# Experts of layers 1 and 3: results gathered in eight pieces over two queues, constant products in two gaps of TensorE, bias additions signalled one by one

## The chip, the cores and the metric

The kernel runs on one core of one Trainium2 chip. The metric is the device time of a whole execution in microseconds (us); each kernel is timed in several executions, and the median is quoted. The engines are named as in the profile: PE is TensorE (matmuls; PEld are its weight loads), DVE is VectorE, ACT is ScalarE, POOL is GpSimd, and SP is the sync engine, which here only issues transfers. SPq is SP's own sequence of transfer issues.

## What is computed

The program is a four-layer perceiver. Each layer has cross-attention, self-attention and a feed-forward part, each added to the token matrix `x` (1024 tokens of 256 numbers). The change touches the feed-forward parts of layers 1 and 3, which are mixtures of experts:

```python
def _L1_ffn_ref(x, gate_w, gate_b, w1, b1, w3, b3, w2, b2, sw1, sb1, sw3, sb3, sw2, sb2):
    def swiglu(x):                       # even and odd columns
        g = jnp.minimum(x[..., ::2], 7.0); l = jnp.clip(x[..., 1::2], -7.0, 7.0)
        return g * jax.nn.sigmoid(1.702 * g) * (l + 1.0)
    scores = jax.nn.softmax(xt @ gate_w.T, axis=-1)
    _, idx = jax.lax.top_k(scores + gate_b, 2)
    ...
    # each chosen expert, weighted with its score:
    h = swiglu((xt @ ew1 + eb1) * (xt @ ew3 + eb3))
    acc + ce[:, None] * (h @ ew2 + eb2)
    # and for every token the shared expert:
    shared = swiglu((xt @ sw1 + sb1) * (xt @ sw3 + sb3)) @ sw2 + sb2
```

Layer 3 has six experts of the form `gelu(x @ W1 + b1) @ W2 + b2`, two for each token, with weights from a softmax over the two largest gate values.

## The kernel before

The 1024 tokens are 8 tiles of 128 rows (`NT = 8`). One class, `SortedExperts`, holds the expert parts of layers 0, 1 and 3. It sorts the (token, expert) pairs by expert into tiles of 128 rows that each belong to one expert, runs the tiles one after the other, stores each tile's result row by row into a matrix in HBM (`out_dram`, by an indirect transfer from POOL), and at the end loads that matrix back in the order of the tokens (`gathered`). In layers 1 and 3 a token has K = 2 results, which PE sums with diagonal matrices of the weights (`sum_pairs`). Layer 1 (names `l1f_...`, kind `swiglu`) has 8 turns for the shared expert (n = 0 to 7, S = 8) and then 23 sorted tiles; layer 3 (`l3f_...`, kind `gelu`) has sorted tiles alone. Layer 0 (`l0f_...`, kind `glu`) has K = 1. Three sets of buffers (`RING = 3`) rotate.

Every engine runs its own instructions in the order in which the code writes them, and semaphores join them. There is no planner. The parts that matter:

- PE, `tensor`: each turn transposes the next tile's rows, multiplies with the first matrices (`up`, L1034; in layer 1 two halves u = 0 and 1 of 32 recorded matmuls each, every half with its own wait), and then does the last product of the turn before (`down`, L1045). The first half of `up` waits for `gate_done` of the turn before, the second for its `hidden_done`. After the loop one `down` is left, and then `sum_pairs` (L1070) sums the pairs of tokens' tiles, g = 0 to 3, each waiting for its own part of the gather.
- ACT, `scalar`: for kind `swiglu` and each half, four additions of a bias (L1111, `side`, 128x128 each), after which one semaphore step tells DVE that all four are done; then the sigmoid (L1116).
- DVE, `vector`: four products (L1155) that read PE's result and `side`, then `gated` (L1160) for u = 0, or L1162, L1163 and `hidden` (L1166) for u = 1. It copies the result of `down` out (L1138), and after the last turn adds the sums to `X` (L1185); in layer 1 it takes the statistics of the next normalization behind each.
- SP, `load`: the experts' weights, two transfers for a tile, and after the last three stores have landed the gather in four transfers (L970), each of 128 x 4 x 256 numbers, that is 512 KB. In layer 3 SP then stores the output in four parts (L3731).
- `keep_busy(bank, n)` (L81) issues n products of constants of 256 columns on PE, whose result nobody reads. At the two places of this change there are none before.

A matmul of 32-bit floats is recorded twice, so that a call of `nc.tensor.matmul` is two records.

## Time and profile before

| | us |
|---|---|
| median of three executions | 2022.7 |
| lowest and highest | 2019.74, 2023.64 |
| the profiled execution, its own time | 2023.79 |
| the profiled execution, its span | 2022.0 |
| PE busy in the span | 1821.4 (90%) |
| DVE, ACT, POOL busy | 1083.4, 815.1, 546.6 |

All times of rows are microseconds from the start of the span. The profile has a page of totals; the trace behind it gives the instructions in order of time (timeline), the waits by pair, and sums over chosen stretches. A timeline row has start, duration, engine, line, operation, what it writes and reads, how many records it merges, and in brackets how long the engine sat idle before it and what released it. A duration of several records is from the start of the first to the end of the last. In rows of stretches, "PEclk" is the granted clock of PE as a share: 1.00 is 2.4 GHz and 0.50 is 1.2 GHz. The page's chain of the work that ended last names many lines of all layers with 1% of the span or less each, so it points to no single one.

### The profile page before, as it was taken

Reading aid. Unit: us, or ns where it says so; the run is one execution under the profiler, and the core shown is the slowest. Engines: PE = TensorE matmul, PEld = TensorE weight load, DVE = VectorE, ACT = ScalarE, POOL = GpSimd, SP = SyncE. Lnnn points to the kernel's source line nnn. Section 1 sums busy time; section 2 is a strip of 40 time slices with the busy share of each in tenths; the row PEclk is TensorE's granted clock in tenths of the full one; section 3 lists DMA queues with packets and bytes.
Section 4 is the critical chain, followed back from the end, with each engine's and each line's share of the span. In section 5 each row is a group of like instructions: output and inputs, shape, how many; then the busy total and the mean of one; then the engine's idle time right before and its main releaser. Section 6 shows DMA issues by size and latency. Waiting matters only on the chain. (4 is left out here: it accounts for less than half of the span.)

```text
span 2022.0 us, 42986 instructions
## 1 busy us (share of the span) xinstructions
PE 1821.4 (90%) x16746; PEld 1409.5 (70%) x16746; DVE 1083.4 (54%) x2711; ACT 815.1 (40%) x2356; POOL 546.6 (27%) x598
## 2 busy tenths in 40 slices
PE   8999779999999888899999799996688899996887
PEld 6886569745777746799999667775444577664786
DVE  7887841451466348675555445557733655355411
ACT  6663521131366243233333245552501566525231
POOL 4441213100244113201121023331202466412241
PEclk9999779999999999999999899998788999997898
DMA  4210069560243000143989331111102355200396
GB/s 142 59 50 4 3 237 319 169 206 31 66 102 101 16 41 3 52 173 131 332 331 333 131 131 49 49 33 43 40 15 68 104 156 157 64 1 2 120 341 224
DMA packets 86882, 233.93 MB, mean 116 GB/s; under 512 B 9648, under 2 KB 45008, under 8 KB 80176
## 3 DMA queue, kind: packets, MB, share of 16 engines
q1 hardware_dynamic: 81040, 216.01, 31.9%
q0 software_dynamic: 5664, 15.47, 2.4%
q8 instruction: 120, 1.97, 0.4%
q14 instruction: 58, 0.48, 0.1%
HBM read 216.23 MB, written 12.07 MB: 113 GB/s over the span
## 5 line engine op out<-in xcount | busy, mean ns | idle before, releaser
L2166 POOL TENSOR_TENSOR l1x_probs<-l1x_probs,l1x_total 128x512 f32<-128x512 f32 x64 | 65.1, 1038 | 209.5 <-DVE l1x_total L2391 209.5
L1487 PE MATMUL PS<-weights,l0x_ctxT 128*128 128x256 f32 x512 | 121.6, 388 | 0.0
L1034 PE MATMUL PS<-l1f_xT,l1f_slot 128*128 128x128 f32 x1024 | 117.0, 275 | 0.0
L1034 PEld LDWEIGHTS PS<-l1f_xT,l1f_slot 128*128 128x128 f32 x1024 | 115.7, 192 | 0.1
L1487 PEld LDWEIGHTS PS<-weights,l0x_ctxT 128*128 128x128 f32 x512 | 94.6, 191 | 15.4 <-issue 2.7
L2898 POOL TENSOR_TENSOR l2x_probs<-l2x_probs,l2x_total 128x512 f32<-128x512 f32 x64 | 65.1, 1038 | 137.2 <-DVE l2x_total L3072 137.2
L235 ACT ACTIVATE std<-moments,eps 128x8 f32<-128x8 f32 x13 | 3.9, 301 | 220.5 <-DVEq L173 135.3
L81 PE MATMUL PS<-consts 128*128 128x256 f32 x276 | 73.9, 423 | 16.1 <-PEq L87 16.1
L81 PEld LDWEIGHTS PS<-consts 128*128 128x128 f32 x276 | 57.8, 214 | 28.7 <-issue 19.9
L1155 DVE SCALAR_TENSOR_TENSOR l1f_product<-PS,l1f_slot,l1f_side 128x128 f32<-128x128 f32 x128 | 36.0, 344 | 65.9 <-ACT l1f_side L1111 65.9
L3362 PE MATMUL PS<-l3x_keysT,l3x_QW 128*128 128x289 f32 x256 | 67.7, 407 | 1.7 <-issue 1.7
L3222 PE MATMUL PS<-weights,HT 128*128 x128 | 59.5, 620 | 9.5 <-DVE X L3255 9.5
L988 POOL DMA_INDIRECT l1f_out_dram<-l1f_out,l1f_sort_target_row x23 | 22.7, 986 | 162.1 <-DVE l1f_out L1138 162.1
L1034 PE MATMUL PS<-HT,weights 128*128 128x128 f32 x512 | 61.5, 282 | 2.2 <-DVE l1f_hidden L1166 1.3
L1034 PEld LDWEIGHTS PS<-HT,weights 128*128 128x128 f32 x512 | 60.5, 198 | 3.2 <-DVE l1f_hidden L1166 1.7
L2925 PE MATMUL PS<-l2x_ctxT,weights 128*128 128x257 f32 x256 | 62.3, 387 | 0.0
L3386 PE MATMUL PS<-tagged,l3x_QT 128*128 128x256 f32 x256 | 60.6, 379 | 1.9 <-ACT tagged L3471 1.9
L1155 DVE SCALAR_TENSOR_TENSOR l1f_product<-PS,weights,l1f_side 128x128 f32<-128x128 f32 x120 | 33.8, 344 | 52.5 <-ACT l1f_side L1111 52.5
L1667 ACT ACTIVATE l0x_sq<-PS 128x256 f32<-128x256 f32 x128 | 47.8, 385 | 32.6 <-PE PS L1487 32.6
L2933 PE MATMUL PS<-weights,l2x_ctxT 128*128 128x256 f32 x256 | 60.4, 379 | 0.0
L3018 ACT ACTIVATE l2x_probs<-PS,l2x_top 128x257 f32<-128x257 f32 x128 | 59.2, 482 | 1.6 <-DVE l2x_top L3066 1.3
L2208 PE MATMUL PS<-HT,weights 128*128 128x512 f32 x128 | 57.3, 608 | 2.2 <-DVE l1x_AT L2355 2.2
(659 smaller groups left out, 4652.6 us busy)
## 6 DMA issues: line engine op xcount, KB each, us to landing
l1f_slot<-in_experts_up_dram SPq DMA_DIRECT2D x16, 2056.0 KB, 10.3
weights<-in_experts_up_dram SPq DMA_DIRECT2D x8, 2056.0 KB, 10.6
weights<-in_experts_down_dram SPq DMA_DIRECT2D x21, 640.0 KB, 5.8
weights<-in_experts_up_dram SPq DMA_DIRECT2D x10, 1024.0 KB, 7.8
l1f_slot<-in_experts_down_dram SPq DMA_DIRECT2D x16, 640.0 KB, 5.2
l0x_ctxT<-in_ctxT_dram SPq DMA_DIRECT2D x32, 257.0 KB, 2.6
l1x_ctxT<-in_ctxT_dram SPq DMA_DIRECT2D x32, 257.0 KB, 3.0
l2x_ctxT<-in_ctxT_dram SPq DMA_DIRECT2D x32, 257.0 KB, 2.6
```

The source lines that it names most:

```text
L81: self.nc.tensor.matmul(self.PS[:, bank, 0:2 * P], self.ident, self.consts[:, 0:2 * P], start=True, stop=True)
L1034: done = nc.tensor.matmul(PS[:, bank + a, m * P:(m + 1) * P], mat[:, c, m * P:(m + 1) * P], x, start=(c == 0), stop=(c == 1))
L1155: done = nc.vector.scalar_tensor_tensor(p[:, m, :], PS[:, 2 * u + 1, m * P:(m + 1) * P], w["b3"][:, 4 * u + m:4 * u + m + 1], self.side[u] ...
L1487: last = nc.tensor.matmul(PS[:, 2 * (b % 2) + k, half * D:(half + 1) * D], ctxT[b % SLOTS][:, c, half * P:(half + 1) * P], kw[:, c, k * D: ...
L2166: nc.gpsimd.tensor_tensor(p, p, bcast(total[b % 2][:, 2 * n:2 * n + 2], 2, KEYS), ALU.mult).then_inc(probs_done, 1)
L2898: nc.gpsimd.tensor_tensor(p, p, bcast(total[b % 2][:, 2 * n:2 * n + 2], 2, 2 * P), ALU.mult).then_inc(probs_done, 1)
L2925: last = nc.tensor.matmul(PS[:, 4 + 2 * o, 0:CTX], wk[:, c, o * P:(o + 1) * P], ctxT[b % 2][:, c, :], start=(c == 0), stop=(c == 1))
L2933: last = nc.tensor.matmul(PS[:, 5, half * D:(half + 1) * D], ctxT[b % 2][:, c, half * P:(half + 1) * P], wv[:, c, :], start=(c == 0), stop ...
L3018: done = nc.scalar.activation(probs[b % 2][:, u, :], PS[:, u, 0:CTX], ACT.Exp, bias=top[b % 2][:, u:u + 1], scale=-1.0, accum_out=total[b ...
L3222: last = nc.tensor.matmul(PS[:, t % 4, :], core.HT[:, c, t * P:(t + 1) * P], experts[:, c, bass.ds(i * (2 * D), 2 * D)], start=(c == 0), s ...
L3362: done = nc.tensor.matmul(PS[:, 2 * (b % 2) + u, 0:KEYS], QW[:, c, b, 4 * u:4 * u + 4, :].rearrange("p h q -> p (h q)"), keysT[b % 2][:, c ...
L3386: nc.tensor.matmul(PS[:, 6 + c, 0:2 * P], tokens[b % 2][:, half, c * P:(c + 1) * P], probsT[b % 2][:, half, :], start=(half == 0), stop=False)
```

## The change

Four things are changed. The gather is issued as eight transfers of one token tile each in layers 1 and 3 (two of the matrix's 128-row blocks, 256 KB), the even ones by SP and the odd ones by ACT, which has a queue of its own; both first wait for the last three stores. `sum_pairs` waits for each token tile instead of each pair of tiles. PE issues 5 constant products before the last `down` of layer 1, and 12 before `sum_pairs` in both layers, into bank 5. ACT signals each of the four bias additions, and DVE waits for each before the product that reads it. Layer 0 keeps its four transfers of 256 KB from SP.

```diff
-        self.gather_done = [sem(f"gather_done{g}") for g in range(4)]
+        self.gather_done = [sem(f"gather_done{g}") for g in range(4 * choices)]
...
+        self.gather_rows(sp, range(0, NT, 2) if self.K == 2 else range(NT // 2))
+
+    def gather_rows(self, eng, parts):
+
+        by_token = self.out_dram[0:self.K * NT * P, :].rearrange("(n p) d -> p n d", p=P)
         for n in range(self.N - RING, self.N):
-            sp.wait_ge(self.stored[n % RING], 16 * self.nth(*divmod(n, RING)))
-        by_token, n = self.out_dram[0:self.K * NT * P, :].rearrange("(n p) d -> p n d", p=P), 2 * self.K
-        for g in range(NT // 2):
-            sp.dma_start(self.gathered[:, n * g:n * (g + 1), :], by_token[:, n * g:n * (g + 1), :]).then_inc(self.gather_done[g], 16)
+            eng.wait_ge(self.stored[n % RING], 16 * self.nth(*divmod(n, RING)))
+        for g in parts:
+            eng.dma_start(self.gathered[:, 2 * g:2 * (g + 1), :], by_token[:, 2 * g:2 * (g + 1), :]).then_inc(self.gather_done[g], 16)
...
-        self.over(pe, lambda: S or flip_rows(0, 0), turn, lambda: down(*divmod(self.N - 1, RING), False))
+        def finish():
+            if self.kind == "swiglu":
+                self.core.keep_busy(5, 5)
+            down(*divmod(self.N - 1, RING), False)
+
+        self.over(pe, lambda: S or flip_rows(0, 0), turn, finish)
         if self.K == 2:
+            self.core.keep_busy(5, 12)
             self.sum_pairs(pe)
...
-            pe.wait_ge(self.gather_done[g], 16)
             for t in (2 * g, 2 * g + 1):
+                pe.wait_ge(self.gather_done[t], 16)
...
-                        done = nc.scalar.activation(self.side[u][:, m, :], PS[:, 2 * u, m * P:(m + 1) * P], ACT.Identity, bias=w["b1"][:, 4 * u + m:4 * u + m + 1])
-                    done.then_inc(self.side_done, 1)
+                        nc.scalar.activation(self.side[u][:, m, :], PS[:, 2 * u, m * P:(m + 1) * P], ACT.Identity,
+                                             bias=w["b1"][:, 4 * u + m:4 * u + m + 1]).then_inc(self.side_done, 1)
...
-                    dve.wait_ge(self.side_done, 2 * n + (u + 1))
                     for m in range(4):
+                        dve.wait_ge(self.side_done, 8 * n + (4 * u + m + 1))
```

`ex.gather_rows(act, range(1, NT, 2))` is written at the end of ACT's program in `l1_feed_forward` (behind `norm.load_table`) and in `l3_feed_forward` (behind `ex.scalar`).

The order of instructions shows where these stand. Line numbers of the kernel after are 4 or 10 higher than those of before; the names of semaphores in brackets are those of their first users, since their numbers are used again by later layers.

PE at the end of layer 1's experts, before:

```order
L1045 MATMUL PS<-l1f_slot,l1f_hidden 128x256 [waits l0x_x_copied,l0x_q_flipped,l0x_q_shifted]
L1045 MATMUL PS<-l1f_slot,l1f_hidden 128x256 x3
L1045 MATMUL PS<-l1f_slot,l1f_hidden 128x256 [waits l0x_x_rows,l0x_q_flipped,l0x_q_shifted]
L1045 MATMUL PS<-l1f_slot,l1f_hidden 128x256 x3
L1070 MATMUL PS<-l1f_gathered,l1f_diagonal 128x256 [waits l0x_q_copied,l0x_scale_ready]
L1070 MATMUL PS<-l1f_gathered,l1f_diagonal 128x256 x3
L1070 MATMUL PS<-l1f_gathered,l1f_diagonal 128x256 [waits l0x_att_done]
L1070 MATMUL PS<-l1f_gathered,l1f_diagonal 128x256 x3
```

and the same place after:

```order
L1049 MATMUL PS<-l1f_slot,l1f_hidden 128x256 [waits l0x_x_copied,l0x_q_flipped,l0x_q_shifted]
L1049 MATMUL PS<-l1f_slot,l1f_hidden 128x256 x3
L81 MATMUL PS<-consts 128x256 x5
L1049 MATMUL PS<-l1f_slot,l1f_hidden 128x256 [waits l0x_x_rows,l0x_q_flipped,l0x_q_shifted]
L1049 MATMUL PS<-l1f_slot,l1f_hidden 128x256 x3
L81 MATMUL PS<-consts 128x256 x12
L1080 MATMUL PS<-l1f_gathered,l1f_diagonal 128x256 [waits l0x_q_copied,l0x_scale_ready]
L1080 MATMUL PS<-l1f_gathered,l1f_diagonal 128x256
L1080 MATMUL PS<-l1f_gathered,l1f_diagonal 128x256 [waits l0x_att_done]
L1080 MATMUL PS<-l1f_gathered,l1f_diagonal 128x256
```

The constant products wait for nothing and stand ahead of the two waiting products; a pair sum now waits before every second of its matmuls instead of every fourth. In layer 3 the end is the same without the five products.

DVE in the first shared turn of layer 1, before:

```order
L1155 SCALAR_TENSOR_TENSOR l1f_product<-PS,weights,l1f_side 128x128 [waits l0x_q_scaled,l1f_shared_biased]
L1155 SCALAR_TENSOR_TENSOR l1f_product<-PS,weights,l1f_side 128x128 x3
L1160 TENSOR_SCALAR l1f_gated<-l1f_product 128x512 [waits dve_step]
L1155 SCALAR_TENSOR_TENSOR l1f_product<-PS,weights,l1f_side 128x128 [waits l0x_q_scaled,l0x_left_done]
L1155 SCALAR_TENSOR_TENSOR l1f_product<-PS,weights,l1f_side 128x128 x3
```

and after:

```order
L1165 SCALAR_TENSOR_TENSOR l1f_product<-PS,weights,l1f_side 128x128 [waits l0x_q_scaled,l1f_shared_biased]
L1165 SCALAR_TENSOR_TENSOR l1f_product<-PS,weights,l1f_side 128x128 [waits l0x_q_scaled] x3
L1170 TENSOR_SCALAR l1f_gated<-l1f_product 128x512 [waits dve_step]
L1165 SCALAR_TENSOR_TENSOR l1f_product<-PS,weights,l1f_side 128x128 [waits l0x_q_scaled,l0x_left_done]
L1165 SCALAR_TENSOR_TENSOR l1f_product<-PS,weights,l1f_side 128x128 [waits l0x_q_scaled] x3
```

Each of the four products now has its own wait on the count of the bias additions; nothing changed its place. In the turns that run as a loop (18 of the 23 sorted tiles) each wait also has a register operation ahead of it.

ACT at the end of layer 1's experts, after (before, the branch follows the second row):

```order
L218 ACT_TABLE_LOAD
L218 ACTIVATE warm<-eps 128x1 [waits eps_set]
L974 DMA l1f_gathered<-l1f_out_dram 128x2x256 [waits l0x_left_zeroed,l0x_one_ready,l0x_left_ready]
L974 DMA l1f_gathered<-l1f_out_dram 128x2x256 x3
L2739 UNCONDITIONAL_BRANCH
```

The four issues of ACT stand behind all of its other work of the layer, with the same three waits that SP has.

## Rows read from the trace of the kernel before

**Rows 1.** Stretches: width, PE, PEld, DVE, ACT, POOL busy (records), PEclk, transfers' share, GB/s

```profile
1100.00:1120.00 20.00, 20.00 (x167) 19.49 (x166) 11.31 (x29) 6.57 (x20) 1.97 (x2) 1.00 0.92 347
1138.50:1141.30 2.80, 2.80 (x7) 1.69 (x6) 0.00 (x0) 0.00 (x0) 0.67 (x1) 0.50 0.13 47
```

**Rows 2.** Timeline of the shared turns 0 and 1 in layer 1: DVE and PE

```profile
857.98 1.13 DVE L1155 SCALAR_TENSOR_TENSOR l1f_product<-PS,weights,l1f_side 128x128 f32<-128x128 f32 x4 [1.90 <-ACT l1f_side L1111]
861.08 3.84 PE L1034 MATMUL PS<-HT,weights 128*128 128x128 f32 x32 [0.35 <-DVE l1f_hidden L1166]
865.85 1.13 DVE L1155 SCALAR_TENSOR_TENSOR l1f_product<-PS,weights,l1f_side 128x128 f32<-128x128 f32 x4
867.50 3.84 PE L1034 MATMUL PS<-HT,weights 128*128 128x128 f32 x32 [0.85 <-DVE l1f_gated L1160]
869.23 1.12 DVE L1155 SCALAR_TENSOR_TENSOR l1f_product<-PS,weights,l1f_side 128x128 f32<-128x128 f32 x4 [1.79 <-ACT l1f_side L1111]
872.33 3.84 PE L1034 MATMUL PS<-HT,weights 128*128 128x128 f32 x32 [0.99 <-DVE l1f_hidden L1166]
```

**Rows 3.** Timeline from the last turn of layer 1 to its last statistics

```profile
1133.11 1.89 PE L1045 MATMUL PS<-l1f_slot,l1f_hidden 128*128 128x256 f32 x8
1133.31 1.14 ACT L1111 ACTIVATE l1f_side<-PS,l1f_slot 128x128 f32<-128x128 f32 x4
1134.55 1.12 DVE L1155 SCALAR_TENSOR_TENSOR l1f_product<-PS,l1f_slot,l1f_side 128x128 f32<-128x128 f32 x4 [2.05 <-ACT l1f_side L1111]
1138.02 3.29 PE L1045 MATMUL PS<-l1f_slot,l1f_hidden 128*128 128x256 f32 x8 [3.02 <-DVE l1f_hidden L1166]
1144.54 2.03 SPq L970 DMA_DIRECT2D l1f_gathered<-l1f_out_dram  x4
1148.24 9.07 PE L1070 MATMUL PS<-l1f_gathered,l1f_diagonal 128*128 128x256 f32 x32 [6.92 <-DMA l1f_gathered<-l1f_out_dram]
1152.03 0.69 DVE L1185 TENSOR_TENSOR X<-PS,X 128x512 f32<-128x512 f32 x1 [10.25 <-PE PS L1070]
...
1158.86 0.25 DVE L206 BATCH_NORM_AGGREGATE moments<-stats 128x2 f32<-128x6 f32 x2
```

**Rows 4.** Timeline of the end of layer 3

```profile
2000.19 1.97 PE L1045 MATMUL PS<-weights,l3f_hidden 128*128 128x256 f32 x8 [0.56 <-issue]
2005.38 2.03 SPq L970 DMA_DIRECT2D l3f_gathered<-l3f_out_dram  x4
2009.48 8.54 PE L1070 MATMUL PS<-l3f_gathered,l3f_diagonal 128*128 128x256 f32 x32 [7.33 <-DMA l3f_gathered<-l3f_out_dram]
```

**Rows 5.** Gather of layer 1: issue to landing; stretches before the pair sums end

```profile
DMA to landing us min/median/max: 3.6/5.6/7.2
...
1145.50:1152.50 7.00, 4.26 (x11) 3.45 (x12) 0.47 (x1) 0.00 (x0) 0.00 (x0) 0.53 0.90 301
1148.30:1151.90 3.60, 3.60 (x9) 2.85 (x10) 0.00 (x0) 0.00 (x0) 0.00 (x0) 0.50 1.00 331
```

**Rows 6.** The page's group of DVE's products in layer 1: busy us, mean ns | idle before

```profile
L1155 DVE SCALAR_TENSOR_TENSOR l1f_product<-PS,l1f_slot,l1f_side 128x128 f32<-128x128 f32 x128 | 36.0, 344 | 65.9 <-ACT l1f_side L1111 65.9
```

**Rows 7.** Timeline of a late sorted turn of layer 1

```profile
1117.09 7.31 PE L1034 MATMUL PS<-l1f_xT,l1f_slot 128*128 128x128 f32 x64
1118.93 0.69 DVE L1166 TENSOR_TENSOR l1f_hidden<-l1f_product,l1f_sigmoid 128x512 f32<-128x512 f32 x1
```

**Rows 8.** Constant products at full clock, timeline of PE ahead of layer 1's experts

```profile
834.89 1.46 PE L81 MATMUL PS<-consts 128*128 128x256 f32 x6
```

**Rows 9.** Two other gaps of PE and the clock in and after them

```profile
1899.30 2.06 PE L816 MATMUL PS<-l3f_sort_marked,l3f_gathered 128*128 128x42 f32 x10 [2.29 <-DVE l3f_gathered L809]
...
1899.30:1902.00 2.70, 2.70 (x14) 2.70 (x15) 2.70 (x15) 0.00 (x0) 0.00 (x0) 0.57 1.02 347
838.67 2.95 PE L262 MATMUL PS<-consts,tagged 128*128 128x128 f32 x16 [2.32 <-DVE tagged L186]
...
838.60:840.90 2.30, 2.23 (x12) 1.39 (x12) 2.30 (x8) 0.59 (x1) 2.01 (x5) 1.00 0.98 281
```

More of the change, by code:

```diff
@@ L2788, in _ @@
             norm.load_table(act)
+            ex.gather_rows(act, range(1, NT, 2))
         @block.vector
@@ L3762, in _ @@
             ex.scalar(act)
+            ex.gather_rows(act, range(1, NT, 2))
         @block.vector
```

## The prediction

> **What bounds the kernel now.** I read the stretches first. Inside layer 1's experts PE is the bound: in a late stretch of 20 us it is busy for all 20, at the full clock [rows 1]. So a signal that reaches DVE earlier is worth nothing there; I look for places where PE itself waited. The timeline has two kinds. In the shared turns 0 to 2 of layer 1 PE stood still three times, for 0.35, 0.85 and 0.99 us, each time for a result of DVE that hangs on ACT's bias additions [rows 2]. And at the end of each expert part PE stands in an open chain: last hidden values, last down product, its copy and store, gather, pair sums [rows 3, 4]. In layer 1 PE waited 3.02 us for the hidden values, then did the last down product in 3.29 us, where the same product took 1.89 us one turn before [rows 3]; the granted clock was 0.50 in that stretch [rows 1], that is 1.2 GHz instead of 2.4. Then it waited 6.92 us for the gather and summed in 9.07 us, again at 0.50 for most of the first half [rows 3, 5]. Layer 3 is the same at the end, with a last down product at full speed (1.97 us), a wait of 7.33 us and sums of 8.54 us [rows 4]. Layer 0 is left as it is.
>
> **Part 1, bias additions one by one, shared turns.** ACT's four additions take 1.14 us and DVE's four products 1.12 us, one behind the other [rows 3]. When each product waits only for its own addition, the last one starts where the first starts now and the other three lie beside ACT: the last product now starts (4 - 1) x 0.26 us behind the first (1.12 less the 0.34 of one, over three steps [rows 6]), so each chain that begins with PE is shorter by 0.78 us. The first stall of PE (0.35) needs 0.35 of that and goes whole. The second waits for `gated` of turn 1, whose chain began behind DVE's sorting work without any idle time [rows 2], so it takes over the 0.78 of the turn before: 0.85 shrinks to 0.07, and the running gain is 0.78. The third waits for `hidden` of turn 1, behind a sigmoid that is 0.78 earlier and a product row that again waited for ACT [rows 2]: the chain is 1.56 earlier, PE's own first half only 0.78, so 0.78 of the 0.99 goes. Running gain **1.56 us**. Bounds: 0.35, if only the first stall goes, and 2.19, all three. I take 1.56, since it follows from the chain. After this PE never waits until the last turn, so what is won is kept. Cost in the sorted turns: in the row of a late turn `hidden` was done at 1119.62 (1118.93 + 0.69), and PE needs it at the second half of `up`, 1117.09 + 3.6 = 1120.7 [rows 7]. That slack of 1.1 us, plus the 0.78, covers four waits with their register operations per half.
>
> **Part 2, last turn of layer 1.** The same 0.78 us comes off the chain from ACT's additions (1133.31) to the down product (1138.02) [rows 3]. Here nothing hides it: **0.78 us** (bounds 0 and 0.78).
>
> **Part 3, five constant products before the last down product.** Six records took 1.46 us [rows 8] and eight took 1.89 [rows 3], so a record costs 0.215 us at the full clock. Five calls are ten records, 2.15 us, from 1134.84 (1133.11 + 8 x 0.215) to 1137.0. The hidden values release PE at 1138.02 - 0.78 = 1137.24. They fit, with 0.25 us to spare; if the price is off or the wait shorter they delay the product by what is over. The product should then run as layer 3's does after a short wait, in 1.97 us [rows 4] instead of 3.29: **1.32 us** (bounds 0, the clock falls all the same, and 1.40, the 1.89 of a turn before).
>
> **Part 4, twelve constant products before the pair sums.** 24 records are 5.16 us and begin right behind the last down product, so they end well inside waits of 6.92 and 7.33 us [rows 3, 4]: they delay nothing. They leave PE idle for 6.92 - 5.16 = 1.8 us in layer 1 and 7.33 - 5.16 = 2.2 in layer 3. If the clock holds, the pair sums take 1.89 + 24 x 0.215 = 7.05 us: 9.07 - 7.05 = 2.02 and 8.54 - 7.05 = 1.49. Two things could be late next. The transfers: the fourth issue began at about 1146.1 (four in 2.03 us from 1144.54 [rows 3]), and its part landed some 7.2 us later, at 1153.3 [rows 5], 8.8 us behind the first issue; the sums would start 3.7 us after the issue (1148.24 - 1144.54), and end 10.75 after it, so the last pair (1.89 us) needs its data at 8.9. That just fits. And DVE: its work from the first addition to the last statistics took 7.08 us [rows 3]; it can start 3.70 + 1.89 after the issue, and ends at 12.7 instead of 14.57 (1159.11 - 1144.54). So layer 1 keeps **1.9 us** and layer 3, where DVE only adds, **1.5 us**. Bounds for each: 0 (the clock falls in the gap) and these.
>
> **Part 5, eight pieces on two queues.** The wait per token tile lets PE begin when 256 KB are there. But with two queues pieces 0 and 1 start together, and the 16 engines of the transfers are full while the gather flows: share 1.00 at 331 GB/s, 301 over its whole length [rows 5]. If they share evenly, each of two pieces lands when the old 512 KB did: gain 0. If piece 0 comes first, up to half a part: 256 KB at 301 GB/s is 0.87 us, in each layer. I take **0**; the last pair of pieces ends at the same time either way. SP's issues took 2.03 us for four parts [rows 3], and they were over (1146.57) long before the data (1152.5) [rows 5], so a second issuer shortens nothing at the end. ACT's own work of the layer is over when it comes to its issues, and nothing is queued behind them but the next layer. The Trainium skill speaks of this in "DMA: Bandwidth & Descriptors": under "Issuing engines are not separate DMA queues" it says that transfers started by several engines run on the same 16 and only the issuing time is saved, and under "Queues, rings and completion order" that each of these engines takes turns between the queues, packet by packet. The share of 1.00 agrees with the first; no run here shows the second. By these the gain of part 5 is 0, and by the row alone it is open between 0 and 0.87.
>
> **Sum.** 1.56 + 0.78 + 1.32 + 1.9 + 1.5 = 7.06 us. The profiled execution had a time of 2023.8 us and a span of 2022.0; with this it would have 2016.7 and 2014.9. The median of the runs shown is 1.1 us lower than the profiled time, 2022.7, and from that I forecast **2015.7 us**.
>
> **The rivals.**
>
> A. *The clock falls in the gap that the twelve products leave* (the products do not do what they are for). PE's gaps of this size went both ways: after 2.32 us at 838.67 the clock stayed 1.00, after 2.29 us at 1899.30 it was at 0.57 on average in the next 2.7 us [rows 9]. Layer 3's gap of 2.2 us is of that size, layer 1's 1.8 us shorter. One fall in layer 3 costs 1.5, one in layer 1 up to 1.9: 2017.2, 2017.6, and 2019.1 for both.
>
> B. *Pieces come staggered and the sums start early.* 0.87 us more in each layer, as far as transfers and DVE let it through: 7.06 + 1.7 = 8.8, **2013.9 us**. For it: SP and ACT can issue a little apart. Against: full engines.
>
> C. *Single waits do not overlap.* If DVE's products each pay more than ACT's pace, the chains of parts 1 and 2 shorten by little; with the lower bounds 0.35 and 0 the sum is 5.1, **2017.6 us**. Against it: DVE's products are 0.34 us long at a pace of 0.26, ACT's pace is 0.26 too.
>
> D. *Slower: two queues of 1 KB packets get in each other's way.* ACT's queue is used nowhere before, so no row prices it. Parts 1 to 3 bring 3.66 us. The change turns slower when each gather's end moves back by over 1.83 us; slower by over 0.2% (4.05 us) when by 3.9. With the rate halved to 150 GB/s the 2.1 MB need 14 us instead of 7, and the last piece lands 7 us later; against sums that now end 4.0 us behind the last landing (1157.3 - 1153.3) and then 1.9 behind, each layer loses 4.9: 2022.7 + 9.8 - 3.66 = **2028.8 us**. Against it: POOL's stores ran beside SP's loads in the stretch of 347 GB/s [rows 1].
>
> **Chances and range.** 0.2% is 4.05 us, about what a measurement of this kernel can tell from no change. The forecast (2015.7, both clocks held) 0.47; A 0.25; B 0.12; C 0.10; D 0.06. The range takes in A with both falls below and B above: 2013.9 to 2019.1, and a little at the lower end, because every shift in time changes where elsewhere the clock falls, and the three executions before differ by 3.9 us: **2012.5 to 2019.2**. A, B and C, but for A with both falls at once together with such a shift, all stay over 4.05 us faster: faster 0.84, within 0.2% 0.12, slower 0.04.
>
> **What would show it right or wrong.** (1) The three stalls in the shared turns: 0, about 0.1 and 0.2 us. (2) DVE's four products start about 0.4 us behind ACT's first addition instead of 1.24. (3) The last down product of layer 1 at 1.9 to 2.0 us, right behind constant products that end before it is released, PEclk 1.00. (4) Pair sums of about 7.05 us in both layers, first one 3.6 to 4.1 us after the first issue, clock 1.00; 8.5 to 9 us would be A. (5) From the first issue to the last landing 8.8 us as before; over 10.6 would be D, and a first landing at under 3.2 us B. It would be wrong if PE had new waits in the sorted turns of layer 1, or if the clock changed its falls in other layers by more than what is won.

## The result and the profile after

The changed kernel ran at a median of 2014.49 us (8 executions, 2009.49 to 2016.19) against 2021.45 for the kernel before (8 executions, 2019.52 to 2025.42): 6.96 us less. The ratio is 0.9963, with a 95% interval of 0.9950 to 0.9976. The profiled execution took 2014.46 us with a span of 2012.7.

The timeline of the shared turns of layer 1, PE only (start, duration, engine, line, what it writes and reads, records, idle time before and what ended it), answers [rows 2]:

```profile
857.65 0.33 PE L735 MATMUL PS<-l1f_chosen,consts 128*128 128x64 f32 x2
...
858.04 7.36 PE L1038 MATMUL PS<-HT,weights 128*128 128x128 f32 x64
865.24 1.89 PE L1049 MATMUL PS<-weights,l1f_hidden 128*128 128x256 f32 x8
867.84 3.84 PE L1038 MATMUL PS<-HT,weights 128*128 128x128 f32 x32 [0.70 <-DVE l1f_gated L1170]
871.90 3.84 PE L1038 MATMUL PS<-HT,weights 128*128 128x128 f32 x32 [0.22 <-DVE l1f_hidden L1176]
875.57 1.89 PE L1049 MATMUL PS<-weights,l1f_hidden 128*128 128x256 f32 x8
```

The first stall is gone: 64 records stand in one row. The other two are 0.70 and 0.22 us. From the product of L735, which stands behind turn 0's `up`, to the down product of turn 1 it is 17.92 us. The same two points in the timeline of the kernel before are 19.46 us apart (the second row is turn 0's down product):

```profile
856.54 0.33 PE L735 MATMUL PS<-l1f_chosen,consts 128*128 128x64 f32 x2
...
864.75 1.89 PE L1045 MATMUL PS<-weights,l1f_hidden 128*128 128x256 f32 x8
...
876.00 1.89 PE L1045 MATMUL PS<-weights,l1f_hidden 128*128 128x256 f32 x8
```

The end of layer 1's experts answers [rows 3]:

```profile
1134.36 1.89 PE L1049 MATMUL PS<-l1f_slot,l1f_hidden 128*128 128x256 f32 x8
1134.56 1.14 ACT L1121 ACTIVATE l1f_side<-PS,l1f_slot 128x128 f32<-128x128 f32 x4 [0.92 <-PE PS L1038]
1135.03 1.13 DVE L1165 SCALAR_TENSOR_TENSOR l1f_product<-PS,l1f_slot,l1f_side 128x128 f32<-128x128 f32 x4 [2.05 <-ACT l1f_side L1121]
...
1136.09 2.32 PE L81 MATMUL PS<-consts 128*128 128x256 f32 x10
...
1138.51 1.97 PE L1049 MATMUL PS<-l1f_slot,l1f_hidden 128*128 128x256 f32 x8
...
1140.31 5.34 PE L81 MATMUL PS<-consts 128*128 128x256 f32 x24
...
1143.71 1.92 SPq L974 DMA_DIRECT2D l1f_gathered<-l1f_out_dram  x4
1143.73 2.02 ACTq L974 DMA_DIRECT2D l1f_gathered<-l1f_out_dram  x4
1146.79 3.69 PE L1080 MATMUL PS<-l1f_gathered,l1f_diagonal 128*128 128x256 f32 x16 [1.13 <-DMA l1f_gathered<-l1f_out_dram]
...
1150.74 3.72 PE L1080 MATMUL PS<-l1f_gathered,l1f_diagonal 128*128 128x256 f32 x16 [0.27 <-DMA l1f_gathered<-l1f_out_dram]
...
1156.02 0.25 DVE L206 BATCH_NORM_AGGREGATE moments<-stats 128x2 f32<-128x6 f32 x2
```

DVE's first product starts 0.47 us behind ACT's first addition, where it was 1.24. The constant products end just before the last down product, which now takes 1.97 us. PE's gap (idle time) before the sums is 1.13 us, and the sums run at full speed with one wait of 0.27 for a piece. The end of layer 3 answers [rows 4]:

```profile
1994.49 5.34 PE L81 MATMUL PS<-consts 128*128 128x256 f32 x24
...
1997.87 1.92 SPq L974 DMA_DIRECT2D l3f_gathered<-l3f_out_dram  x4
...
2001.52 7.14 PE L1080 MATMUL PS<-l3f_gathered,l3f_diagonal 128*128 128x256 f32 x32 [1.69 <-DMA l3f_gathered<-l3f_out_dram]
```

Stretches of the changed kernel (busy times of PE, PEld, DVE, ACT, POOL, then the granted clock, the transfers' share and GB/s), and the landing times of layer 1's gather, answer [rows 1] and [rows 5]:

```profile
1100.00:1120.00 20.00, 20.00 (x166) 19.49 (x165) 11.33 (x29) 6.94 (x21) 1.97 (x2) 1.00 0.92 351
1134.00:1142.00 8.00, 7.90 (x39) 6.73 (x38) 3.70 (x9) 2.63 (x6) 1.75 (x2) 1.00 0.06 19
...
1147.00:1154.00 7.00, 6.73 (x31) 5.61 (x31) 4.54 (x13) 0.00 (x0) 0.00 (x0) 1.00 0.61 203
2001.50:2008.50 7.00, 6.98 (x32) 5.99 (x32) 2.08 (x3) 0.00 (x0) 0.00 (x0) 1.00 0.82 271
...
DMA to landing us min/median/max: 2.9/5.5/7.0
```

The clock is 1.00 in each of these stretches. Place by place, in us, each number the difference of two starts or ends in the rows above and in [rows 2 to 4]:

| stretch | before | after | difference | forecast |
|---|---|---|---|---|
| shared turns, L735 to the down product of turn 1 | 19.46 | 17.92 | -1.54 | -1.56 |
| last turn of layer 1, ACT's first addition to the last down product | 4.71 | 3.95 | -0.76 | -0.78 |
| that down product | 3.29 | 1.97 | -1.32 | -1.32 |
| layer 1, first issue of the gather to the last statistics | 14.57 | 12.56 | -2.01 | -1.9 |
| layer 3, first issue of the gather to the end of the sums | 12.64 | 10.79 | -1.85 | -1.5 |
| sum | | | -7.48 | -7.06 |

The column of the kernel before is one profile, the same one that the forecast was made from. The spans differ by 9.3 us, so 1.8 us of this pair of profiles lies elsewhere. It is a balance of three parts. Up to L735 the changed kernel is 1.1 us later. In the sorted turns of layer 1 it loses 1.7 us. From the last statistics of layer 1 to the gather of layer 3 it gains 4.7 us, of which 2.9 are shorter waits of PE for the weights of layer 3's experts. The waits of that stretch by pair (total us, times, longest), first before, then after:

```profile
PE PS L1034 <- DMA weights<-in_experts_up_dram: 5.6, 4, 2.2
PE PS L1034 <- DMA l3f_slot<-in_experts_up_dram: 1.3, 2, 0.9
```

```profile
PE PS L1038 <- DMA weights<-in_experts_up_dram: 2.0, 5, 1.0
PE PS L1038 <- DMA l3f_slot<-in_experts_up_dram: 2.0, 2, 1.3
```

The 1.7 us that layer 1 loses are a fall of the clock, in the down product behind the narrow product of L816 (46 columns). The same stretch, first before, then after:

```profile
897.00:900.30 3.30, 3.30 (x24) 3.09 (x24) 1.47 (x6) 2.81 (x9) 0.00 (x0) 1.00 0.00 0
```

```profile
897.00:900.30 3.30, 3.30 (x8) 2.57 (x9) 2.24 (x6) 1.82 (x7) 0.00 (x0) 0.50 0.00 0
```

PE is busy all the time in both, but does 8 records instead of 24. Up to this point the two programs differ in their signals alone. The fall stands in 4 of the 14 profiles of this document. All 4 have single signals, but so have 11 of the 14, so whether the signals make it likelier can't be told.

### The profile page after: what moved, and what is told of

It is laid out like the page before. It is cut to its first block and busy times, and to the rows that moved or that the text cites. A ratio compares the mean times of both kernels' runs of the same rounds, so it can differ in the third digit from the quotient of the medians.

```text
span 2012.7 us, 43220 instructions
## 1 busy us (share of the span) xinstructions
PE 1827.7 (91%) x16804; PEld 1416.5 (70%) x16804; DVE 1084.5 (54%) x2711; ACT 815.4 (41%) x2356; POOL 547.6 (27%) x598
## 3 DMA queue, kind: packets, MB, share of 16 engines
q8 instruction: 120, 1.97, 0.4%
## 5 line engine op out<-in xcount | busy, mean ns | idle before, releaser
L81 PE MATMUL PS<-consts 128*128 128x256 f32 x334 | 85.9, 412 | 15.9 <-PEq L87 15.9
L81 PEld LDWEIGHTS PS<-consts 128*128 128x128 f32 x334 | 68.0, 207 | 29.7 <-issue 19.7
L1121 ACT ACTIVATE l1f_side<-PS,l1f_slot 128x128 f32<-128x128 f32 x128 | 36.5, 368 | 66.0 <-PE PS L1038 66.0
```

The lines of the kernel that those rows point to most:

```text
L81: self.nc.tensor.matmul(self.PS[:, bank, 0:2 * P], self.ident, self.consts[:, 0:2 * P], start=True, stop=True)
```

## The experiments

Three groups of four kernels ran, each group on one chip with its own runs of the kernel before: 2021.13 (22 executions), 2020.82 (16) and 2020.22 us (25). I call the stretch from the first issue of the gather to the last statistics of layer 1 E1, and that from the first issue to the end of the sums of layer 3 E3; they stand in the table above with 14.57 and 12.64 before and 12.56 and 10.79 after. The median of the changed kernel differed by up to 3.5 us between groups, so a part worth 2 us is read from its stretch and only checked by the median. One more number shows why. If the five stretches of the table are taken out of a profile's span, the rest should be the same for all kernels. Over the 14 profiles it went from 1959.3 to 1972.8 us: 1967.3 and 1966.7 in the two of the kernel before, 1962.5 to 1966.1 in the three of the changed kernel. A profile's own total therefore says nothing about a part of 1 to 4 us.

### The changed kernel again

No edit.

> The changed kernel once more, as the yardstick of this group. If what it gains lies at the places of the change, the pair sums of layers 1 and 3 again take 7.1 to 7.7 us at full clock and the last down product of layer 1 takes 1.97 us, while the falls of the clock in other places stand elsewhere than in the first profile. If instead the gain was a lucky position of the clock, the time is back near 2019 to 2022. My theory: 2013 to 2016 us, about 7 us under the kernel before.

2015.14 us (7 executions), ratio 0.9961 (0.9947 to 0.9974). E1 was 12.54 and E3 10.90, the gaps before the sums 1.66 and 1.61 us. E1 and E3 repeat to 0.1 us.

### Without the twelve constant products

```diff
         if self.K == 2:
-            self.core.keep_busy(5, 12)
             self.sum_pairs(pe)
```

> The changed kernel without the twelve constant products before the pair sums (layers 1 and 3); everything else stays. Theory (the products keep the clock up through the wait for the gather): PE idles about 6.3 us, the clock falls, the first half of the pair sums runs at 1.2 GHz, and the sums take 8.5 to 9.1 us in both layers instead of 7.7 and 7.1; 1.4 to 2 us are lost in each, some 3 us in all: about 3 us over the changed kernel. Rival (the pieces' earlier landing is what counts, the clock recovers anyway): under 1 us is lost.

2020.21 us (12 executions), 5.1 over the changed kernel of the group; the ratio to the kernel before is 0.9996 (0.9986 to 1.0006). Timeline and a stretch of this kernel:

```profile
1142.81 9.25 PE L1079 MATMUL PS<-l1f_gathered,l1f_diagonal 128*128 128x256 f32 x32 [6.79 <-DMA l1f_gathered<-l1f_out_dram]
1999.21 9.42 PE L1079 MATMUL PS<-l3f_gathered,l3f_diagonal 128*128 128x256 f32 x32 [6.83 <-DMA l3f_gathered<-l3f_out_dram]
...
1142.80:1147.00 4.20, 4.19 (x10) 3.36 (x11) 0.40 (x1) 0.00 (x0) 0.00 (x0) 0.50 1.05 345
```

The sums start at 1.2 GHz and take 9.25 and 9.42 us; E1 is 14.60 and E3 13.03, 2.1 us more in each, 4.2 in all, where 3 was expected. The expectation was right in kind and too low in size. Whether the finer pieces still give something without the products depends on the profile they are held against: the kernels with four pieces and no products had E1 and E3 of 14.57 and 12.64, of 16.21 and 13.90, and of 14.91 and 13.40 (the first profile of the kernel before, its second and that of the signals alone, both below). Two things don't close. The profiled execution took 2014.52 us, the lowest of the 12, in spite of its long sums, because the rest of its span was short (1961.1). And by the places this kernel keeps 3.3 us of the gain (7.5 less 4.2), where the median keeps 0.9 and its interval at most 2.8. What the other executions lost beyond the places was not profiled.

### One signal for four bias additions

```diff
-                        nc.scalar.activation(self.side[u][:, m, :], PS[:, 2 * u, m * P:(m + 1) * P], ACT.Identity,
-                                             bias=w["b1"][:, 4 * u + m:4 * u + m + 1]).then_inc(self.side_done, 1)
+                        done = nc.scalar.activation(self.side[u][:, m, :], PS[:, 2 * u, m * P:(m + 1) * P], ACT.Identity, bias=w["b1"][:, 4 * u + m:4 * u + m + 1])
+                    done.then_inc(self.side_done, 1)
...
-                    for m in range(4):
-                        dve.wait_ge(self.side_done, 8 * n + (4 * u + m + 1))
+                    dve.wait_ge(self.side_done, 2 * n + (u + 1))
+                    for m in range(4):
```

> The changed kernel with one signal behind four bias additions again, and DVE waiting once for all four. Theory: PE's three stalls in the shared turns come back (0.35, 0.85, 0.99 us; with the change 0, 0.70, 0.22), and the last turn's chain is 0.78 us longer: 2.3 us over the changed kernel, 1.54 of it between the first shared turn and the third, and nothing in the sorted turns. Rival (single waits cost in the sorted turns, with their register operations, and give part of the gain back): the sorted turns become shorter without them, and the loss is under 1 us.

2016.19 us (9 executions), 1.05 over the changed kernel. The timeline of the shared turns, PE:

```profile
855.41 0.33 PE L735 MATMUL PS<-l1f_chosen,consts 128*128 128x64 f32 x2
...
859.94 3.84 PE L1038 MATMUL PS<-HT,weights 128*128 128x128 f32 x32 [0.35 <-DVE l1f_hidden L1176]
...
866.37 3.84 PE L1038 MATMUL PS<-HT,weights 128*128 128x128 f32 x32 [0.86 <-DVE l1f_gated L1170]
871.20 3.84 PE L1038 MATMUL PS<-HT,weights 128*128 128x128 f32 x32 [1.00 <-DVE l1f_hidden L1176]
874.88 1.89 PE L1049 MATMUL PS<-weights,l1f_hidden 128*128 128x256 f32 x8
```

All three stalls are back, and from 855.41 to 874.88 it is 19.47 us, as in the kernel before. In the last turn the down product starts 4.72 us behind ACT's first addition:

```profile
1132.18 1.14 ACT L1121 ACTIVATE l1f_side<-PS,l1f_slot 128x128 f32<-128x128 f32 x4
1136.90 1.97 PE L1049 MATMUL PS<-l1f_slot,l1f_hidden 128*128 128x256 f32 x8 [0.87 <-DVE l1f_hidden L1176]
```

So the part is worth 1.54 + 0.77 = 2.3 us at its places. The median shows 1.05 of it; with 7 and 9 executions the rest is within what the remainder of the span moves. E1 and E3 stayed at 12.52 and 10.85: the sums' gain does not hang on the signals.

### Four pieces from one queue

```diff
-        self.gather_rows(sp, range(0, NT, 2) if self.K == 2 else range(NT // 2))
+        self.gather_rows(sp, range(NT // 2))
...
-            eng.dma_start(self.gathered[:, 2 * g:2 * (g + 1), :], by_token[:, 2 * g:2 * (g + 1), :]).then_inc(self.gather_done[g], 16)
+            eng.dma_start(self.gathered[:, n * g:n * (g + 1), :], by_token[:, n * g:n * (g + 1), :]).then_inc(self.gather_done[g], 16)
...
-            for t in (2 * g, 2 * g + 1):
-                pe.wait_ge(self.gather_done[t], 16)
+            pe.wait_ge(self.gather_done[g], 16)
+            for t in (2 * g, 2 * g + 1):
```

> The changed kernel with the gather as before: four transfers of 512 KB, all from SP, and one wait for each pair of token tiles; constant products and single signals stay. Theory (the transfers' engines are full, so pieces and queues change only the start): the sums begin 3.7 us (layer 1) and 4.1 us (layer 3) behind the first issue instead of 3.1 and 3.65, and end at most 0.5 us later than with eight pieces; the total is 0.3 to 1 us higher than that of the changed kernel. The idle time of PE ahead of the sums grows to about 1.8 and 2.2 us, and in one or the other the clock may fall, which would add 1.5 to 1.9 us. Rival (two queues move the data faster): the sums end 1.5 us later or more in each layer with the clock at 1.00.

2014.64 us (7 executions), as the changed kernel in the group (2015.14), so by the median the finer pieces and the second queue gave nothing. But the profiled execution (2016.2 us) shows what can happen. Timeline and stretches:

```profile
1144.54 8.83 PE L1081 MATMUL PS<-l1f_gathered,l1f_diagonal 128*128 128x256 f32 x32 [2.05 <-DMA l1f_gathered<-l1f_out_dram]
...
2001.59 8.83 PE L1081 MATMUL PS<-l3f_gathered,l3f_diagonal 128*128 128x256 f32 x32 [2.29 <-DMA l3f_gathered<-l3f_out_dram]
...
1142.00:1144.50 2.50, 0.48 (x3) 0.08 (x1) 0.00 (x0) 0.00 (x0) 0.00 (x0) 1.00 0.99 323
1144.90:1148.00 3.10, 3.10 (x9) 2.48 (x8) 0.07 (x1) 0.00 (x0) 0.00 (x0) 0.51 1.04 342
```

The sums begin 4.0 and 4.2 us behind the first issue, PE's gap is 2.05 and 2.29 us, and the clock, 1.00 in the gap, is at 0.51 once the sums have begun. E1 is 14.63 and E3 13.07: both parts of the gain in the sums are gone in this execution, with the twelve products in place. The expectation of an end at most 0.5 us later failed here, and the fall that it allowed for one layer came in both. How often that happens in the other executions the median can't tell: the 4.3 us would be hidden by what the rest of the span moves, and no second profile was taken.

### Four pieces with sixteen constant products

```diff
-            self.core.keep_busy(5, 12)
+            self.core.keep_busy(5, 16)
```

on top of the four pieces.

> Four pieces of 512 KB from SP as in the run with four pieces, but 16 constant products before the pair sums instead of 12, so that PE's gap is 0.3 to 0.6 us instead of 2.05 and 2.29. Theory (what was lost with four pieces was the clock, which fell in those gaps): the clock stays at 1.00, the sums take 7.05 to 7.2 us instead of 8.83 in both layers, and end 11.1 to 11.4 us behind the first issue, 0.3 to 0.6 later than with eight pieces. Rival (the pair wait and the late start cost, not the clock): the sums end at 12.8 to 13.1 again.

```profile
1149.01 7.14 PE L1081 MATMUL PS<-l1f_gathered,l1f_diagonal 128*128 128x256 f32 x32 [0.32 <-DMA l1f_gathered<-l1f_out_dram]
2009.50 7.14 PE L1081 MATMUL PS<-l3f_gathered,l3f_diagonal 128*128 128x256 f32 x32 [0.33 <-DMA l3f_gathered<-l3f_out_dram]
```

With gaps of 0.32 and 0.33 us the sums take 7.14 us; E1 is 12.94 and E3 11.16. So what four pieces had lost was the clock, and four pieces at full clock are 0.3 to 0.4 us slower than eight in each layer, by the later first landing. The total, 2018.37 us (11 executions, 2012.94 to 2023.00; ratio 0.9984, 0.9970 to 0.9998), is some 4 us above what the changed kernel's ratio would give, and the places explain 0.7 of it. In the profiled execution (2022.44 us) the rest of the span took 1972.8 us, the longest of all profiles, at a granted clock of 0.949 over the whole span against 0.954 in the changed kernel's first profile. Why this kernel was slower elsewhere is open.

### Eight pieces from one queue

```diff
-        self.gather_rows(sp, range(0, NT, 2) if self.K == 2 else range(NT // 2))
+        self.gather_rows(sp, range(NT) if self.K == 2 else range(NT // 2))
...
-            ex.gather_rows(act, range(1, NT, 2))
```

> The changed kernel with all eight pieces of 256 KB issued by SP, in order, ACT issuing none. Theory (the transfers' engines are full, a second queue only saves issue time): eight issues of some 0.47 us take 3.8 us, still under the 7 us of the data; piece 0 is no longer mixed with piece 1, so the sums begin as early as with two queues or 0.2 to 0.5 us earlier (2.9 to 3.6 us behind the first issue), and end within 0.3 us of 10.75 us behind it. Total within 1 us of the changed kernel. Rival (the second queue is what made it work): first landing at 3.7 us or later, or waits inside the sums, 1 us or more slower in each layer.

2009.94 us (5 executions). The timeline at layer 1:

```profile
1138.50 3.97 SPq L974 DMA_DIRECT2D l1f_gathered<-l1f_out_dram  x8
1141.34 1.97 PE L1080 MATMUL PS<-l1f_gathered,l1f_diagonal 128*128 128x256 f32 x8 [0.88 <-DMA l1f_gathered<-l1f_out_dram]
...
1143.53 5.45 PE L1080 MATMUL PS<-l1f_gathered,l1f_diagonal 128*128 128x256 f32 x24 [0.23 <-DMA l1f_gathered<-l1f_out_dram]
```

The first sum starts 2.84 us behind the first issue, 0.2 us earlier than the earliest start with two queues. E1 was 12.28 and E3 10.52. The second run tells whether this stands:

> The kernel with all eight pieces from SP again, beside the changed kernel on the same chip. In the first run the sums ended 10.5 us behind the first issue in both layers against 10.75 to 10.9 with two queues, which is 0.5 to 0.7 us in all, but the medians of two different groups differed by 4 to 5 us. Theory: the difference at the two places is 0.6 us, the rest was the clock in other places: this kernel 0 to 2 us under the changed kernel. Rival (two queues cost something elsewhere): 3 us or more under it again.

2012.56 us (12 executions) beside 2011.67 for the changed kernel. E1 was 12.69 and E3 11.02, both 0.1 to 0.2 above the changed kernel. So ACT's queue is neither a gain nor a loss that can be seen: E1 12.3 to 12.7 and E3 10.5 to 11.0 with one queue, 12.5 to 12.6 and 10.8 to 10.9 with two. The 4 to 5 us by which the first median lay lower did not repeat; in its profile the rest of the span was the shortest of all (1959.3).

### Fourteen constant products

```diff
-            self.core.keep_busy(5, 12)
+            self.core.keep_busy(5, 14)
```

> The changed kernel with 14 constant products before the pair sums instead of 12. They take 6.0 us and leave gaps of 0.3 to 0.9 us where 12 leave 1.1 to 1.7. Theory (gaps of up to 1.7 us don't let the clock fall, or seldom): sums of 7.1 to 7.7 us as before, no gain in the median, within 1 us of the changed kernel. Rival (in a part of the unprofiled executions the clock does fall in these gaps): the median is 0.5 to 1.5 us lower and the spread smaller.

The gaps were 0.51 and 0.68 us, the sums 7.14 and 7.34, E1 12.26 and E3 10.84: no gain at the places beyond 0.3 us, since with twelve the clock had held as well. Of 5 executions (2010.27 to 2021.3, median 2010.74) the spread is too wide to say whether the median is lower. The profiled one was the slowest, 2021.3, with every place of the change at full clock: its rest of the span took 1972.6 us.

### Without the five constant products

```diff
         def finish():
-            if self.kind == "swiglu":
-                self.core.keep_busy(5, 5)
             down(*divmod(self.N - 1, RING), False)
```

> The changed kernel without the five constant products before layer 1's last down product. With single signals PE's gap there is 3.02 - 0.78 = 2.2 us. Theory: this is about the size at which the clock fell with four pieces (2.05 and 2.29), so it falls in some executions and not in others; where it falls, the last down product takes up to 3.3 us instead of 1.97, where not, 1.97. In the median 0.5 to 1.3 us over the changed kernel. Rival: the shorter gap alone is enough, and nothing is lost.

2013.09 us (6 executions, 2008.95 to 2018.28). In the profiled execution the last down product took 1.97 us:

```profile
1133.81 1.97 PE L1049 MATMUL PS<-l1f_slot,l1f_hidden 128*128 128x256 f32 x8 [2.25 <-DVE l1f_hidden L1174]
```

The gap of 2.25 us did not let the clock fall there. The next kernel has the same gap:

### The signals alone, in the kernel before

The edit of the single signals, as in the change, and nothing else.

> The kernel before with one part of the change alone: each bias addition signalled and waited for by itself, nothing else. Theory: the stretch from the start of layer 1's experts to the end of their last turn becomes 2.3 us shorter where the clock is the same (1.54 in the shared turns, 0.78 in the last turn), the sorted turns keep 9.1 us each, and PE's wait before the last down product goes from 3.02 to 2.2 us, so the clock may stay up there in some executions. Total 2 to 3 us under the kernel before. Rival (of the 7 us of the change this part gives only what the whole medians differ by, 1 us): 2019.5 to 2020.5 us.

2017.02 us (12 executions), 3.2 under the kernel before in its group; ratio 0.9986 (0.9974 to 0.9998). From L735 to the down product of turn 1 it was 17.93 us and in the last turn's chain 3.95, as in the changed kernel, so the 2.3 us are there without anything else of the change. The sums, without products, took 9.19 and 9.24 us, E1 14.91 and E3 13.40. At the last down product:

```profile
1138.62 3.07 PE L1045 MATMUL PS<-l1f_slot,l1f_hidden 128*128 128x256 f32 x8 [2.25 <-DVE l1f_hidden L1166]
...
1138.70:1141.60 2.90, 2.90 (x8) 1.92 (x8) 0.00 (x0) 0.00 (x0) 0.97 (x1) 0.61 0.13 45
```

The same gap of 2.25 us behind the same work, and here the clock fell and the product took 3.07 us. So for a gap of about 2 us its length alone does not decide, and the five products are an insurance worth up to 1.1 us (3.07 less 1.97) once the signals are single, not a fixed gain.

### The yardsticks of the last group

> The changed kernel once more, as the yardstick of this group: 2010 to 2017 us, 6 to 8 us under the kernel before.

2011.67 us (8 executions), ratio 0.9963 (0.9950 to 0.9975); E1 12.61, E3 10.79, gaps 1.72 and 1.69.

> The kernel before, one more profile. The last down product of layer 1 again at about 3.3 us, pair sums of 8.5 to 9.1 us in both layers, and from the last turn of layer 1 to the first work of the next layer 21 us as in the first profile. The places where the clock falls elsewhere, and the waits of layer 3's sorted tiles for weights, may lie otherwise: where they do, they are not of the change.

One execution, 2026.35 us. Its places, from the timeline:

```profile
1142.01 3.62 PE L1045 MATMUL PS<-l1f_slot,l1f_hidden 128*128 128x256 f32 x8 [3.03 <-DVE l1f_hidden L1166]
1153.12 10.16 PE L1070 MATMUL PS<-l1f_gathered,l1f_diagonal 128*128 128x256 f32 x32 [7.48 <-DMA l1f_gathered<-l1f_out_dram]
...
2010.95 9.62 PE L1070 MATMUL PS<-l3f_gathered,l3f_diagonal 128*128 128x256 f32 x32 [7.50 <-DMA l3f_gathered<-l3f_out_dram]
```

The down product took 3.62 us, the sums 10.16 and 9.62: E1 was 16.21 and E3 13.90, 1.6 and 1.3 us above the first profile. Of the 1.6 us in layer 1, 0.55 are a later start of the sums (4.25 us behind the first issue instead of 3.70) and 1.09 longer sums. The expectation (3.3, and 8.5 to 9.1) was too narrow. Without the products, the end of the experts does not have one price; with twelve or fourteen products and eight pieces E1 was 12.3 to 12.7 in all eight profiles.

## Why the prediction was right, point by point

The forecast was 2015.7 us from 2022.7, a gain of 7.0; measured were 6.96, and 6.0 to 8.6 in the other two groups. The first median of before was 1.25 us above the one of eight executions, so the forecast gain was met more closely than the forecast time. That it was met to 0.1 us is luck: the places brought 7.5 us, the pair of profiles 9.3, and the rest of the span moves by more than the whole gain from one profile to another. What the runs bear out is the working, place by place, with the reservations below.

- **Part 1, single signals in the shared turns**: 1.56 forecast, 1.54 measured, and 1.54 again when taken back. One point was booked wrong on the way: the second stall was to shrink to 0.07 us and was 0.70. PE comes to it earlier by what the first stall gave back, and the stall shrinks by only the rest. The first stall gave back more than its 0.35: turn 0's down product starts 7.59 us behind L735 instead of 8.21, 0.62 less, since its 64 records of `up` now take 7.36 us in one run. That leaves 0.15 of the 0.77. The running gain of 0.78 that the same step stated was right: 10.19 us from L735 to the second stall's end instead of 10.96. Sorted turns: PE is busy all 20 us of 1100 to 1120 with 166 records, where it was 167, and from the down product of turn 1 to ACT's first addition of the last turn it is 257.3 us in both profiles of the kernel before and in two of the three of the changed one (the third, 259.0, has the fall behind L816). So the single waits themselves cost nothing there. Rival C fell.
- **Part 2**: 0.78 forecast, 0.76 measured.
- **Part 3**: 1.32 forecast and measured. The products delayed nothing: the down product starts 4.15 us behind the one before it with them (1134.36 to 1138.51) and 4.15 without them (1129.66 to 1133.81). But the working took for granted that without them the clock falls; at the shortened gap of 2.25 us it fell in one profile and held in another.
- **Part 4, clock in the sums**: 1.9 and 1.5 forecast, 2.01 and 1.85 measured. The sums took 7.05 us by the forecast, 7.14 in layer 3, and in layer 1 7.41 of records and one wait of 0.27, since they began earlier than the data could keep up with. The gaps were to be 1.8 and 2.2 us and were 1.13 to 1.72. Rival A did not come about in the changed kernel: three profiles, six gaps, clock at 1.00 each time. It did come about with four pieces, at 2.05 and 2.29, in the one profile taken. That kernel has just what this part reckoned with, sums that begin when the old 512 KB have landed. So that the clock held was not shown by the working of this part; it leaned on the earlier landing, which part 5 put at nothing.
- **Part 5, pieces and queues**: 0 was taken, between 0 and 0.87. By the first run the sums start 0.62 and 0.45 us earlier, in layer 3 all of which reaches the end, in layer 1 it goes into the wait for a piece. With four pieces at full clock E1 and E3 are 0.3 to 0.4 us longer. So the term was mis-sized by 0.3 to 0.4 in each layer, and what the step missed may be the larger effect: the earlier landing shortens PE's gap by 0.3 to 0.9 us, and in every profile with the shorter gap the clock held. In layer 1 of the first profile the first piece landed after 2.9 us, which by the prediction's own sign (under 3.2) was rival B; the other five gathers of the changed kernel had 3.4 to 3.5. B's full 0.87 us came nowhere. That ACT's queue adds nothing was forecast and holds.
- **Rival D**: the last piece, issued some 1.5 us behind the first, lands 7.0 us later, at 1143.7 + 1.5 + 7.0 = 1152.2, 8.5 us behind the first issue where it was 8.8. Two queues do not get in each other's way. The turns between queues that the Trainium skill describes ("DMA: Bandwidth & Descriptors", "Queues, rings and completion order") would let pieces 0 and 1 land nearly together. The trace agrees with that in part: with two queues the first piece of SP landed 2.9 to 3.6 us behind its issue and that of ACT 3.4 to 4.1, 0.5 us later in each of 14 gathers, while with one queue the first landed after 2.7 to 3.1. So the second queue does hold up piece 0, but not as long as piece 1; no run shows turns packet by packet.

## What to carry to other kernels

Where TensorE stands in an open wait of known length before latency-bound work, it can pay to fill most of the wait with constant products: here, taking the twelve out lost 4.2 us at their places and 5.1 us of the median, of a gain of some 7. How far to fill is a question of how often the clock falls in what is left. In the nine profiles with eight pieces and twelve or fourteen products, or with four pieces and sixteen, the 18 gaps were 0.32 to 1.75 us and the clock held in all; at 2.05 to 2.29 us, at the same places, it fell three times and held once. Transfers in finer pieces were worth 0.3 to 0.4 us by themselves, and more where the earlier landing shortens such a gap. A signal for each of several short operations pays only in turns in which the chain through them is what the bound engine waits for; here it paid 0.78 us in each such chain and nothing in the sorted turns.

## What the runs showed of the hardware that I had not expected

The same kernel's open end had two prices: the last down product took 3.29 and 3.62 us, the sums 9.07 and 10.16 in layer 1, in two profiles. A gap of PE of 2.25 us behind the same work let the clock fall in one kernel and not in another. And the clock fell to 1.2 GHz with PE busy without a break, behind 32 records of 46 columns: from 897.0 to 900.3 it was 0.50 in one profile and 1.00 in the other, for the same work, and the fall cost 1.7 us in each of the 4 profiles of 14 that have it. Falls of the clock and waits for the weights of layer 3's experts (1.6 to 6.9 us in a profile) both move the rest of the span, which differed by up to 13.5 us between profiles. The medians of the changed kernel, of 7 and 8 executions, differed by 3.5 us between groups (2015.14 and 2011.67).
